# Layer 1's output projection: one 32-bit product replaced by three products of halves, the low half of its moving-side rows made on GpSimd

## What is computed

```
normed = layer_norm(x, w, b)
k, v   = normed @ Wk.T, normed @ Wv.T
r      = sigmoid(normed @ Wr.T)
state  = 0.95 * state + 0.05 * k * v      # one step of a recurrence for each token
y      = r * state                        # the gated values
x      = x + y @ Wo.T                     # the output projection
```

## Time and profile before

| | value |
|---|---|
| median of three runs | 1246.59 us |
| the profiled execution's own time | 1253.09 us |
| its span, first to last instruction | 1251.2 us |
| PE busy | 1119.2 us (89%) |
| DVE busy | 917.4 us (73%) |
| POOL busy | 700.2 us (56%) |
| ACT busy | 622.4 us (50%) |
| mean granted clock of TensorE | 0.958 of full |

### The profile page before, as it was taken

One profiled execution on the slowest core, in us unless ns is written; L12 is line 12 of the kernel. 1 busy time (PEld: TensorE's weight loads), 2 busy tenths in 40 slices (PEclk: granted clock), 3 DMA queues, 4 the chain that ended last, 5 costly groups with the idle time before them and its releaser, 6 DMA issues. The chain is left out here.

```text
span 1251.2 us, 22912 instructions
## 1 busy us (share of the span) xinstructions
PE 1119.2 (89%) x6916; PEld 989.3 (79%) x6916; DVE 917.4 (73%) x2031; ACT 622.4 (50%) x1027; POOL 700.2 (56%) x572
## 2 busy tenths in 40 slices
PE   6899999999999998758999999999999999999900
PEld 6778777777777776647888888888898999999900
DVE  5688888888888887645676666666677888888736
ACT  4344444444444444234454444545455666666528
POOL 1111544444444444565677667766576777777634
PEclk9899999999999999769999999999999999999965
DMA  4011121111111121255666557655678989899559
GB/s 152 18 51 51 52 52 52 52 51 51 51 51 51 51 51 35 74 172 130 167 158 145 141 146 166 156 142 140 137 188 222 239 233 238 242 229 236 126 173 381
DMA packets 80660, 164.17 MB, mean 131 GB/s; under 512 B 27424, under 2 KB 45600, under 8 KB 80352
## 3 DMA queue, kind: packets, MB, share of 16 engines
q1 hardware_dynamic: 49248, 126.16, 33.5%
q0 software_dynamic: 31360, 37.38, 15.7%
HBM read 118.01 MB, written 45.49 MB: 131 GB/s over the span
## 5 line engine op out<-in xcount | busy, mean ns | idle before, releaser
L1125 POOL DMA_INDIRECT x_acc<-fy_sb,pair_out x142 | 286.4, 2017 | 150.1 <-DVE fy_sb L1226 77.1
L1281 PE MATMUL fring<-fxh,fw_hi 128*128 128x256 f32 (+1 forms) x816 | 265.2, 325 | 3.6 <-DVE fxl L1217 1.9
L1283 PE MATMUL fring<-fxh,fw_lo 128*128 128x256 f32 (+1 forms) x816 | 265.4, 325 | 0.0
L1282 PE MATMUL fring<-fxl,fw_hi 128*128 128x256 f32 (+1 forms) x816 | 265.1, 325 | 0.0
L1144 ACT ACTIVATE fw_hi<-w_raw 128x1024 fp32r<-128x1024 f32 x153 | 161.2, 1054 | 148.0 <-PE fy L1324 139.7
L509 POOL TENSOR_TENSOR rs<-ve,neg_half 128x4 f32<-128x4 f32 x48 | 63.3, 1319 | 261.1 <-DVE nm L596 261.0
L1197 DVE TENSOR_TENSOR fw_lo<-w_raw,fw_hi 128x1024 fp32r<-128x1024 f32 x153 | 186.6, 1219 | 17.3 <-ACT fw_hi L1144 17.2
L88 POOL DMA_INDIRECT xg<-x_src,pair_in x142 | 160.6, 1131 | 43.3 <-issue 42.0
L78 POOL DMA_INDIRECT slot_list<-pairs,slot_u x128 | 140.8, 1100 | 59.3 <-issue 43.6
L1281 PEld LDWEIGHTS fring<-fxh,fw_hi 128*128 128x128 f32 x816 | 153.7, 188 | 17.2 <-ACT fxh L1162 4.1
L832 PE MATMUL ring<-xh,w_hi 128*128 128x512 f32 x384 | 161.8, 421 | 3.2 <-DVE xl L601 2.9
(11 more groups left out here) (135 smaller groups left out, 1972.2 us busy)
## 6 DMA issues: line engine op xcount, KB each, us to landing
w_raw<-w_ffn SPq DMA_DIRECT2D x153, 512.0 KB, 5.0
x_in<-h SPq DMA_DIRECT2D x16, 512.0 KB, 3.3
x_src<-x SPq DMA_DIRECT2D x16, 512.0 KB, 4.3
x_acc<-x SPq DMA_DIRECT2D x16, 512.0 KB, 5.6
acc<-x_acc SPq DMA_DIRECT2D x16, 512.0 KB, 7.5
out<-o SPq DMA_DIRECT2D x16, 512.0 KB, 6.6
xg<-x_src,pair_in POOLq DMA_INDIRECT x142, 3.5
x_acc<-fy_sb,pair_out POOLq DMA_INDIRECT x142, 5.6
```

The costliest lines, as they stand in the source:

```text
L1125: nc.gpsimd.indirect_dma_start(x_acc, bass.IndirectOffsetOnAxis(pair_out[j][:, q, 0:1].bitcast(U32), 0), y[j][:, q, :], None, compute_op=A ...
L1281: nc.tensor.matmul(out, hi, rows_hi, start=dc == 0, stop=False)
L1282: nc.tensor.matmul(out, hi, rows_lo, start=False, stop=False)
L1283: last = nc.tensor.matmul(out, lo, rows_hi, start=False, stop=dc == DC - 1)
```

## The change

The weights of layer 1's output projection are kept as a high and a low half. ACT writes the high half (`w_out_hi`, in place of the 32-bit copy), and DVE computes the low half once, in front of the first step, as one more instruction at the end of `low_weights(0)`. Layer 2 keeps its 32-bit `w_out`.

In each step ACT copies the two halves-by-feature of `y` to float32r (`y_hi`, two instructions behind `x_hi(1)`), and GpSimd subtracts that from `y` (`y_lo`, two instructions: the first behind the fourth scatter and ahead of `rstd(0)`, the second behind `rstd(0)` and ahead of the fifth scatter). `output(0, ...)` then issues three float32r matmuls where it issued one 32-bit product: yh x w_hi, yh x w_lo, yl x w_hi. PE waits for `yh` and `yl` where it waited for `y`, and DVE's `gated` of layer 1 waits for `yh` and `yl` of the chunk before where it waited for the output product.

```diff
             if within(n, 1, CHUNKS):
-                eng.wait_ge(s_po[l], n * 2)
+                if l == 0:
+                    eng.wait_ge(s_yh, n * 2 + e - 1)
+                    eng.wait_ge(s_yl, n * 2 + e - 1)
+                else:
+                    eng.wait_ge(s_po[l], n * 2)
...
-                nc.scalar.activation(w_out[:, l, :, :], w_raw[:, l, :, 3 * D:4 * D], ACT.Copy).then_inc(s_whi[l], 1)
+                nc.scalar.activation((w_out_hi, w_out)[l][:, :, :], w_raw[:, l, :, 3 * D:4 * D], ACT.Copy).then_inc(s_whi[l], 1)
...
+            def y_hi(n, e):
+                act.wait_ge(s_y[0], n * 2 + e + 1)
+                if within(n, 1, CHUNKS):
+                    act.wait_ge(s_po[0], n * 2)
+                nc.scalar.activation(yh[:, e, :], y[0][:, e, :], ACT.Copy).then_inc(s_yh, 1)
...
+                if layer1:
+                    for e in range(DC):
+                        y_hi(s, e)
...
+            def y_lo(n, e):
+                pool.wait_ge(s_y[0], n * 2 + e + 1)
+                pool.wait_ge(s_yh, n * 2 + e + 1)
+                if within(n, 1, CHUNKS):
+                    pool.wait_ge(s_po[0], n * 2)
+                nc.gpsimd.tensor_tensor(yl[:, e, :], y[0][:, e, :], yh[:, e, :].bitcast(F32),
+                                        ALU.subtract).then_inc(s_yl, 1)
...
                 scatter(s, j, 2, 2)
+                if layer1:
+                    y_lo(s, 0)
                 if within(s, 1, CHUNKS - 2):
                     rstd(0, s + 1)
+                if layer1:
+                    y_lo(s, 1)
                 scatter(s, j, 4, 1)
...
+                if l == 0:
+                    dve.wait_ge(s_whi[l], DC + 1)
+                    nc.vector.tensor_tensor(w_out_lo[:, :, :], w_raw[:, l, :, 3 * D:4 * D],
+                                            w_out_hi[:, :, :].bitcast(F32), ALU.subtract).then_inc(s_wlo[l], 1)
...
-                        last = nc.tensor.matmul(out[:, i * D:(i + 1) * D], y[l][:, dc, q * P:(q + 1) * P],
-                                                w_out[:, l, dc, :], start=dc == 0, stop=dc == DC - 1)
+                        if l == 0:
+                            a, b = yh[:, dc, q * P:(q + 1) * P], yl[:, dc, q * P:(q + 1) * P]
+                            nc.tensor.matmul(out[:, i * D:(i + 1) * D], a, w_out_hi[:, dc, :], start=dc == 0, stop=False)
+                            nc.tensor.matmul(out[:, i * D:(i + 1) * D], a, w_out_lo[:, dc, :], start=False, stop=False)
+                            last = nc.tensor.matmul(out[:, i * D:(i + 1) * D], b, w_out_hi[:, dc, :],
+                                                    start=False, stop=dc == DC - 1)
...
                 if layer1:
-                    pe.wait_ge(s_y[0], s * 2 + 2)
+                    pe.wait_ge(s_yh, s * 2 + 2)
+                    pe.wait_ge(s_yl, s * 2 + 2)
```

More of the change, by code:

```diff
@@ L195, in attention_phase @@
         w_lo = sb("w_lo", [P, LAYERS, DC, 3 * D], F32R)
-        w_out = sb("w_out", [P, LAYERS, DC, D])
+        w_out = sb("w_out", [P, DC, D])
+        w_out_hi = sb("w_out_hi", [P, DC, D], F32R)
+        w_out_lo = sb("w_out_lo", [P, DC, D], F32R)
+        yh = sb("yh", [P, DC, CH], F32R)
+        yl = sb("yl", [P, DC, CH], F32R)
         lnp = sb("lnp", [P, 2, LAYERS, DC])
@@ L259, in attention_phase @@
         s_y = [sem("y_ready0"), sem("y_ready1")]
+        s_yh, s_yl = sem("yh_ready"), sem("yl_ready")
         s_po = [sem("out_product0"), sem("out_product1")]
@@ L324, in first_block @@
                     sp.wait_ge(s_whi[l], DC + 1)
-                    sp.wait_ge(s_wlo[l], DC)
+                    sp.wait_ge(s_wlo[l], DC + 1 - l)
                 w_row = sp.value_load(table[0:1, 0, 0:1], min_val=0, max_val=(E - 1) * P)
@@ L840, in output @@
                     for dc in range(DC):
-                        last = nc.tensor.matmul(out[:, i * D:(i + 1) * D], y[l][:, dc, q * P:(q + 1) * P],
-                                                w_out[:, l, dc, :], start=dc == 0, stop=dc == DC - 1)
+                        if l == 0:
[4 more added lines that the diff above has]
+                                                    start=False, stop=dc == DC - 1)
+                        else:
+                            last = nc.tensor.matmul(out[:, i * D:(i + 1) * D], y[l][:, dc, q * P:(q + 1) * P],
+                                                    w_out[:, dc, :], start=dc == 0, stop=dc == DC - 1)
                 last.then_inc(s_po[l], 1)
@@ L884, in _ @@
             pe.wait_ge(s_whi[0], DC + 1)
-            pe.wait_ge(s_wlo[0], DC)
+            pe.wait_ge(s_wlo[0], DC + 1)
             def step(s, half, j):
```

## The result

The kernel after takes 1258.85 us (median of 8 runs, 1257.08 to 1262.99), the kernel before 1246.26 (8 runs, 1243.68 to 1254.3). The recorded ratio is 1.0079 with a 95% interval of [1.0057, 1.0101]; the quotient of the two medians, 1.0101, is its upper end. The forecast of 1245.9 us with a range up to 1254 was wrong: the change costs 7 to 13 us.

The account below looks back on a forecast made before the run. A ring of DVE, POOL, ACT and a PE piece bounds the loop, without layer 1's output product. Loop, step 0 and last steps 0, step 1 -0.7 us: 1245.9 us against the median 1246.59, range 1239 to 1254.

Parts of the forecast that it names:

- Contention of DVE and GpSimd: GpSimd's y_lo holding up DVE: 0 in the loop; in steps 1 to 3 up to 0.3 us each, 1 us in all.
- The sign that was named for a miss: Period moves by more than 0.3 us; DVE's wait ahead of x_lo, xr or g then says which rival it is.
- The wider gaps lower TensorE's clock: Rival: longer PE wait ahead of normed lowers the clock, 1.6 us per fall, +6 to +19 us; chance 0.11.
- the PE piece of the ring: PE's 11.4 us of the 31.26 us loop step, from normed's transposes through layer 2's output to the gates releasing DVE's g.
- The products: Layer 1's output matmuls 0.113 us apart, 0.74 us less PE per step, 11.8 us in all, hidden in waits: gain 0.
- The new instructions on ACT and POOL: y_hi some 0.55 us each, y_lo 1.1 us each, fitting idle time: cost 0 on ACT, slip 0 to 0.1 on POOL.
- GpSimd is slow: Rival: each subtraction takes 2.8 us, pushing rstd late, 1.4 us in some twelve steps, 1263 us; decides from 2.1; chance 0.06.
- The first steps: Steps before the loop: w_out_lo hidden, 0 for step 0, -0.7 us in step 1 from a shorter DVE wait for PE.

Follow-up runs that it names:

- e1: Kernel after, with GpSimd's first y_lo waiting for both halves of y instead of its own: 1253.15 us, ratio 1.0012.
- e9: Kernel before plus one two-input GpSimd subtraction, 128 x 512, on unrelated buffers behind the fourth scatter of each layer 1 step: 1260.59 us.
- e11: Kernel before plus one GpSimd memset of a 128 x 512 scratch tile behind the fourth scatter of each layer 1 step: 1247.45 us.
- e3: Kernel after, with the first subtraction of a step cut to 64 columns and that half's third products reading yh: 1255.46 us, output incomplete.
- e10: Kernel before plus one one-input GpSimd instruction (decay times 1.0 into a scratch tile) behind the fourth scatter of each layer 1 step: 1257.85 us.
- e2: Kernel after without both GpSimd subtractions and the waits for yl, third product reading yh, so the output differs: 1257.78 us, ratio 1.0052.
- e7: Kernel after, with both subtractions moved from GpSimd to DVE, ahead of the router: 1257.4 us, ratio 1.0059.
- e4: Kernel before, with DVE's add_input (u = xr + x) moved behind layer 1's first y: 1233.4 us, ratio 0.985.
- e5: Kernel after with the edits of both e1 and e4: 1236.97 us, ratio 0.9875.
- e6: e1 plus six useless matmuls on PE in the second output call of each step, overwritten by the real ones: 1253.06 us, ratio 1.0005.
- the probes: e9, e10 and e11, the kernel before with one added GpSimd instruction each: 1260.59, 1257.85 and 1247.45 us.

## Why the prediction was wrong

*Contention of DVE and GpSimd.* The step that failed: "In the loop y_lo lies beside statistics and z, so I take 0". The prediction's own two numbers did not allow the 0: y of e=1 done at 227.45 + 0.68 = 228.13, the scatter's end and so the start of y_lo at 228.08. They overlap by 0.05 us. I read that as neighbours; the chip made it a wait for the whole subtraction, 1.8 us eight times, of which 1.4 reached the period. It is this term of the sum, put at nothing, that turned a forecast of no change into a loss of 11.4 us in the loop. The sign that was named for a miss did not work either: no wait ahead of x_lo, xr or g tells of the held y, and the one ahead of g became shorter (0.35 us against 0.62). I had even seen the reverse case (nb 1.08 us under the scan), bounded this one at a whole y_lo, and then looked for it in steps 1 to 3 alone. There, after, y starts less than 0.02 us past y_lo's end (104.10 both) and loses nothing, which is luck and not a margin. One wait (e1) removes the loss, one foreign instruction (e9) makes it.

The Trainium skill (SBUF — State Buffer, section "SBUF: two separate sides") says that the port shared by VectorE and GpSimd is an exclusive lock kept for a whole instruction, and that a VectorE operation with two SBUF inputs collides only with a GpSimd operation that reads SBUF. e9 and e11 agree. e3 and e10 do not in size: y is held for 0.2 us by a subtraction of 0.42 and for 0.5 by an instruction of 1.89, so the lock for a whole instruction is not what these two show. And by the shown starts y (227.74) is ahead of the subtraction (228.37), yet y is the one that waits. That GpSimd's next instruction takes the port while the scatter ahead of it still runs would fit: y starts 0.23 us after the scatter in the unrolled steps and 0.34 to 0.40 in the loop, and in step 0, without a scatter, an overlap of 0.16 us costs nothing. It is only argued; no run here moved y against the scatter by itself, and the profile's spans on POOL are rough.

*The wider gaps lower TensorE's clock.* A rival at 0.11, and real. Its mechanism and place were right, although it is not what made the kernel after slower: waits near 1.9 us ahead of normed, then the PE piece of the ring at the lower level. Falls came in 2 of 8 loop steps (after, e2, e3) or 3 of 8 (e1, e7), all behind waits of 1.88 to 1.94 us, and in none of the steps with 1.74 us or less (all loop steps of before, e4, e5, e6 and the probes, and of the others the first loop step, 1.62 to 1.63, and the step behind the loop, 1.71 to 1.74). I took 1.6 us per fall; e1's long periods are 32.57, 32.93 and 32.53 against 31.2 to 31.7, 1.3 on average. What it has wrong is its price here: in the kernel after it is hidden behind the held y, at most 0.14 us a fall. The reason against it, "the gap is nearer to 1.57", did not hold, since the gap was the forecast's own 1.95 and the clock fell behind it.

*The products.* Right. 0.12 us apart, PE's wait for slot_u is 0.74 to 0.98 (forecast 1.07) and for normed 1.87 to 1.94 in seven loop steps, 1.63 in the first (1.95). The 11.8 us of PE stayed off the path, as forecast: e5, with both losses taken away, is no faster than e4. xr has no wait in the loop.

*The new instructions on ACT and POOL.* Right in that they have room. y_hi takes 0.63 us, not 0.55. y_lo takes 1.29, not 1.1, inside the bounds of 0.48 and 1.63. The rows where the first wait and the second subtraction show it, ACT first:

```profile
230.25 0.63 ACT L406 ACTIVATE yh<-y 128x512 fp32r<-128x512 f32 x1 [4.03 <-DVE y L303]
230.78 1.07 ACT L414 ACTIVATE x1T<-tp 128x512 f32<-128x512 f32 x2
```

*GpSimd is slow.* It is not: 1.29 us is far from 2.1, and e1, with the same subtractions, has five loop periods without a fall of 31.16 to 31.68, on average 31.42 against 31.26 before. At most 0.2 us of a step can be put down to POOL's list.

*The first steps.* -0.7 was forecast up to the loop, -1.2 came (182.83 against 181.65). The xr that takes the product of PE's step 1 waits 0.15 us for PE after the change where the earlier trace rows has 0.73, so 0.6 of the 1.2 is the forecast term. For the rest no cause was isolated; e1, whose first steps hold the same work, starts the loop at 182.41. In step 0 both subtractions were done at 30.96, not 32.4, and PE started at 31.32 against 31.69, released by DVE's bias and not by yl. The clock of the first stage was 0.84 against 0.89, and the loop still started earlier.

*What stays open.* At which moment GpSimd takes the port, why a subtraction of 64 columns or an instruction with one input holds y only in part, and which of several equal waits of PE is followed by a fall of the clock.

## What to carry to other kernels

When work moves to GpSimd, lay its start against the *end* of every VectorE instruction with two SBUF inputs, and take anything short of a clear gap as a possible full collision; here a wait that holds GpSimd back 0.3 us until VectorE is through took the ratio from 1.0079 to 1.0012. Compare durations of unchanged instructions between two traces before looking for waits: a held instruction shows as a longer one. And when matmul time is saved inside a ring that other engines set, what grows is TensorE's idle time, which can be charged a second time in clock, as in e1.

## What the runs showed of the hardware

- A VectorE instruction with two SBUF inputs whose ordinary end lies 0.03 us or more behind the start of a two-input GpSimd instruction of 512 columns, which stands behind an indirect DMA, waits for all of it: 2.41 to 2.49 us instead of 0.68, in 8 of 8 steps. Behind no such DMA an overlap of 0.16 us cost nothing (step 0, one case). Against 64 columns the wait is 0.2 us (e3), against one input 0.5 (e10), against a memset none (e11).
- A GpSimd instruction on 128x512 that reads one input and multiplies by a constant takes 1.89 us in that place and 1.49 to 1.55 in the written-out steps, one with two inputs 1.06, the subtraction of this change (output in fp32r) 1.29, a memset 0.55.
- A wait of 1.88 us of PE was enough for a fall of the granted clock in some steps (223.53), and one of 1.94 in the same kernel (256.21) was not. Which of two such steps falls is not explained by the length of the wait.
